# A transformer-like block of neighbourhood attention and three 3×3 convolutions: eight wait-carrying products dropped, the second convolution in full products plus one tap on row halves, and new orders on three engines

## What is computed

```python
q = jnp.einsum('bhwd,de->bhwe', x, Q_P)
k = jnp.einsum('bhwkd,de->bhwke', stk, K_P)
v = jnp.einsum('bhwkd,de->bhwke', stk, V_P)
scores = jnp.einsum('bhwke,bhwe->bhwk', k, q) * mask
alpha = jax.nn.softmax(scores, axis=-1)
attn = jnp.einsum('bhwk,bhwke->bhwe', alpha, v)
t = x + attn
t_in = t
t = jax.nn.relu(_conv(t, ff1_kernel, ff1_bias))
t = jax.nn.relu(_conv(t, ff2_kernel, ff2_bias))
t = jax.nn.relu(_conv(t, ff3_kernel, ff3_bias))
return t_in + t
```

## Time and profile before

| | |
|---|---|
| median of 3 runs | 2381.85 us (2379.44 to 2382.46) |
| the profiled execution | 2380.99 us, its span 2379.0 us |
| TensorE busy | 2287.5 us, 96% of the span |
| VectorE busy | 1895.5 us, 80% |
| ScalarE busy | 1127.4 us, 47% |
| mean granted TensorE clock | 0.993 of full speed |

### The profile page before, as it was taken

The page is one execution under the profiler, slowest core; times in us unless marked ns, Lnnn a source line. Parts: engine busy times, 40 slices in busy tenths (PEclk is TensorE's granted clock), DMA queues, the critical chain, the costliest instruction groups (busy, mean ns, idle before and its releaser), DMA issues.

```text
span 2379.0 us, 65460 instructions
## 1 busy us (share of the span) xinstructions
PE 2287.5 (96%) x25180; PEld 1317.7 (55%) x25180; DVE 1895.5 (80%) x2851; ACT 1127.4 (47%) x3108; POOL 15.5 (1%) x24
## 2 busy tenths in 40 slices
PE   4999999999999999999999999999998999999998
PEld 2655555555565555555555555555555555555554
DVE  4888888887588888888768888888877888888886
ACT  1554455444454554454345544544535445444543
POOL 2000000000000000000000000000000000000000
PEclk9999999999899999999999999999999999999999
DMA  4444544544355445444344454445434544454443
GB/s 125 138 137 136 158 134 125 160 141 134 94 158 152 137 126 162 139 136 137 123 138 144 126 160 140 135 136 157 135 124 119 156 147 138 127 160 136 128 153 119
DMA packets 291286, 328.79 MB, mean 138 GB/s; under 512 B 89300, under 2 KB 223252, under 8 KB 284564
## 3 DMA queue, kind: packets, MB, share of 16 engines
q1 hardware_dynamic: 291164, 327.17, 46.4%
HBM read 152.50 MB, written 33.82 MB: 78 GB/s over the span
## 4 chain that ended last, share of the span: by engine, by line
PE 79%; DVE 12%; issue 5%; ACT 1%; DVEq 1%; DMA 1%; SPq 0%; ACTq 0%
PE conv_banks L476 28%; PE conv_banks L435 16%; PE conv_banks L490 15%; PE mix_bank L413 6%; PE score_banks L387 3%; DVE work L836 3%; PE score_banks L398 3%; PE mix_bank L425 3%; DVE dt L764 2%; DVE tf L746 2%; DVE dt L760 2%; PE score_banks L381 1%; PE proj_bank L420 1%; PE score_banks L395 1%; PE conv_banks L450 1%
## 5 line engine op out<-in xcount | busy, mean ns | idle before, releaser
L476 PE MATMUL conv_banks<-dodd,w3f 128*64 128x512 f32 (+1 forms) x1656 | 500.3, 579 | 6.2 <-DVE dodd L760 3.9
L476 PE MATMUL conv_banks<-deven,w3f 128*64 128x512 f32 (+1 forms) x1656 | 489.9, 566 | 0.0
L598 ACT ACTIVATE prob<-score_banks,negmax 128x100 f32<-128x100 f32 x1040 | 343.0, 343 | 273.4 <-DVE negmax L726 273.4
L435 PE MATMUL conv_banks<-dt,w1f 128*64 128x256 f32 (+3 forms) x4224 | 414.4, 384 | 0.0
L490 PE MATMUL conv_banks<-duh,w2h 64*128 64x512 f32 (+2 forms) x1632 | 362.2, 423 | 4.0 <-ACT m_sb L634 2.1
L664 ACT ACTIVATE relued<-work,bias 128x1024 f32<-128x1024 f32 (+2 forms) x136 | 150.4, 1108 | 435.7 <-DVE work L836 435.7
L490 PE MATMUL conv_banks<-duh,w2l 64*128 64x512 f32 (+2 forms) x1632 | 329.5, 382 | 0.0
L435 PEld LDWEIGHTS conv_banks<-dt,w1f 128*64 128x64 f32 (+1 forms) x4224 | 219.2, 135 | 138.6 <-issue 65.9
L490 PE MATMUL conv_banks<-dul,w2h 64*128 64x512 f32 (+2 forms) x1632 | 286.4, 383 | 0.0
L476 PEld LDWEIGHTS conv_banks<-dodd,w3f 128*64 128x64 f32 x1656 | 138.8, 137 | 226.5 <-issue 181.3
L490 PEld LDWEIGHTS conv_banks<-duh,w2h 64*128 64x128 f32 x1632 | 168.7, 185 | 137.7 <-issue 104.5
(11 more groups left out here) (97 smaller groups left out, 3224.2 us busy)
## 6 DMA issues: line engine op xcount, KB each, us to landing
xk<-x_keys SPq DMA_DIRECT2D x66, 800.0 KB
xc<-x_bands SPq DMA_DIRECT2D x66, 650.0 KB, 5.0
dodd<-dodd SPq DMA_DIRECT2D x68, 512.0 KB, 5.1
xr<-x_bands SPq DMA_DIRECT2D x264, 128.0 KB, 3.5
out<-work SPq DMA_DIRECT2D x60, 512.0 KB, 2.7
dt<-dt SPq DMA_DIRECT2D x68, 256.0 KB, 2.3
deven<-deven SPq DMA_DIRECT2D x68, 256.0 KB, 5.7
duh<-duh SPq DMA_DIRECT2D x68, 256.0 KB, 2.4
```

What stands on the lines that cost most here:

```text
L435: mm = nc.tensor.matmul(bank[(LOWER, UPPER)[o], n * 256 + lo * 64:n * 256 + hi * 64], w1f[i][rows, m, s, o * C:o * C + C], dt[rows, lo + s ...
L476: return nc.tensor.matmul(bank[rows, lo * 128:hi * 128], w3f[:, m, s, odd * C:odd * C + C], source[:, lo + s // 2:hi + s // 2, m], start=s ...
L598: last = nc.scalar.activation(prob[:, g % 2, a], score_banks[:, g % 2, a * KEYS:(a + 1) * KEYS], ACT.Exp, bias=negmax[:, g % 2, a:a + 1], ...
```

## The change

1. **Waits.** In the loop's steps, the eight products of 2 columns are gone (`hold` keeps them in the prologue only). Their waits became `await_band`, `await_r`, `await_prob` and `await_y`, and stand ahead of a product of a convolution a little before the piece: `await_band` ahead of the last pair of the step before, `await_r(b, 0)` within the first convolution, `await_prob(b, 0)` and `await_r(b, 1)` ahead of the last two taps of a tile of the third, `await_prob(b, 1)` and `await_y` ahead of the last two products of `begin2`.
2. **Second convolution.** `begin2` issues four full products (128 rows) and `end2` two more, then six on row halves (three pairs). `go_on2` and `half_done` are gone.
3. **Orders.** TensorE: the tiles of the third convolution go 0, 1, 2, 3 (before 0, 2, 1, 3), `end2` of tiles 0 and 1 follow their own tile, `v_product` stands between `begin2` of tiles 2 and 3. ScalarE and VectorE: reordered as the diff shows.

Cut to its core, the diff of the helpers and of TensorE is:

```diff
 def fill_of(which, j):
-    return ORDER3.index(j) if which == CONV3 else 4 + 2 * j + (which == EVEN)
+    return j if which == CONV3 else 4 + 2 * j + (which == EVEN)
...
-                nc.tensor.matmul(score_banks[:, 0, 0:2], eye16_sb[:], window_sb[:, 0:2], start=True, stop=True)
...
+            def await_band(b):
+                pe.wait_ge(t_ready, b * 2)
+                pe.wait_ge(xc_in, b * 16 + 16)
+                pe.wait_ge(xs_in, b * 32 + 32)
...
                 for w in (w2h, w2l):
-                    tap2(k, EVEN, j, LOWER, 0, w, duh, w is w2h, False)
-                    tap2(k, ODD, j, UPPER, 0, w, duh, w is w2h, False)
-
-            def go_on2(G, k, j):
-                for w in (w2h, w2l):
-                    tap2(k, EVEN, j, LOWER, 1, w, duh, False, False)
-                    tap2(k, ODD, j, UPPER, 1, w, duh, False, False)
+                    if ahead and w is w2l:
+                        ahead()
+                    tap2(k, EVEN, j, FULL, 0, w, duh, w is w2h, False)
+                    tap2(k, ODD, j, FULL, 1, w, duh, w is w2h, False)
+
+            def end2(G, k, j, ahead=None):
+
                 pe.wait_ge(du_low, G * 2 + (j // 2 + 1))
-                for s in range(2):
-                    even = tap2(k, EVEN, j, LOWER, s, w2h, dul, False, False)
-                    odd = tap2(k, ODD, j, UPPER, s, w2h, dul, False, False)
-                even.then_inc(half_done, 1)
-                odd.then_inc(half_done, 1)
-
-            def end2(G, k, j):
-                pe.wait_ge(half_done, G * 8 + (2 * j + 2))
+                tap2(k, EVEN, j, FULL, 0, w2h, dul, False, False)
+                tap2(k, ODD, j, FULL, 1, w2h, dul, False, False)
                 for n, (w, d) in enumerate(((w2h, duh), (w2l, duh), (w2h, dul))):
-                    odd = tap2(k, ODD, j, LOWER, 1, w, d, False, n == 2)
-                    even = tap2(k, EVEN, j, UPPER, 0, w, d, False, n == 2)
+                    if ahead and n == 2:
+                        ahead()
+                    odd = tap2(k, ODD, j, UPPER, 0, w, d, False, n == 2)
+                    even = tap2(k, EVEN, j, LOWER, 1, w, d, False, n == 2)
...
                 conv3_tile(G, k, 0)
-                conv3_tile(G, k, 2)
+                conv3_tile(G, k, 1, (lambda: await_prob(b, 0)) if att else None)
                 if att:
                     turn(b, 0)
-                conv3_tile(G, k, 1)
+                conv3_tile(G, k, 2, (lambda: await_r(b, 1)) if att else None)
                 if att:
                     scores(b, 1)
                 conv3_tile(G, k, 3)
                 begin2(G, k, 0)
-                go_on2(G, k, 0)
+                end2(G, k, 0)
                 if att:
                     mix(b, 0)
-                begin2(G, k, 1)
-                go_on2(G, k, 1)
+                begin2(G, k, 1, (lambda: await_prob(b, 1)) if att else None)
                 if att:
                     turn(b, 1)
-                end2(G, k, 0)
                 end2(G, k, 1)
                 if att:
                     mix(b, 1)
-                begin2(G, k, 2)
+                begin2(G, k, 2, (lambda: await_y(b)) if att else None)
                 if att:
                     v_product(b)
-                go_on2(G, k, 2)
                 begin2(G, k, 3)
-                go_on2(G, k, 3)
                 end2(G, k, 2)
-                end2(G, k, 3)
+                next_band = None if k == BANDS - 2 else b if k == BANDS - 1 else b + 1
+                end2(G, k, 3, None if next_band is None else lambda: await_band(next_band))
```

In ScalarE's `step`:

```diff
+                if att:
+                    keep_r(b, 0)
                 if k:
                     relu_conv2(G, k - 1, ODD, 1)
-                if att:
-                    keep_r(b, 0)
-                if k:
                     relu_conv2(G, k - 1, EVEN, 1)
+                if att:
+                    keep_r(b, 1)
                 keep_u2(G, k)
                 if att:
                     exps(b, 0)
                     exps(b, 1)
-                    keep_r(b, 1)
+                keep_m2(G, k, CONV3)
                 relu_conv1(G, k)
-                keep_m2(G, k, CONV3)
```

and in VectorE's:

```diff
                 if k:
                     outer(G, k - 1, ODD, 1)
+                if k < BANDS:
+                    t_inputs(None, b - 1, k % 2, 1)
+                if k:
                     outer(G, k - 1, EVEN, 1)
                     inputs(G, k - 1, ODD, 0, 1)
                     inputs(G, k - 1, EVEN, 0, 1)
+                if att:
+                    max_scores(b, 0)
                 middle1(G, k)
                 if att:
-                    max_scores(b, 0)
+                    max_scores(b, 1)
+                outer1(G, k)
+                if att:
+                    scale(b, 0)
+                if k:
+                    inputs(G, k - 1, EVEN, 1, 1)
+                if att:
+                    scale(b, 1)
                 if k:
                     inputs(G, k - 1, ODD, 1, 1)
...
                 if att:
                     scale(b, 2)
+                u_low(G, k, 1)
+                if att:
                     scale(b, 3)
-                u_low(G, k, 1)
```

More of the change, by code:

```diff
@@ L449, in conv1 @@
                     pe.wait_ge(dve_read, outer_read(G, ODD, 1))
-                nc.tensor.matmul(conv_banks[:, 2 * outer, 0:2], eye16_sb[:], window_sb[:, 0:2], start=True, stop=True)
                 streams = (0, 3) if outer else (2, 1)
@@ L453, in conv1 @@
                     for i in range(2):
+                        if att and n == 1 and i == 1:
+                            await_r(b, 0)
                         for o in ((0,) if k == BANDS else (0, 1)):
@@ L589, in _ @@
                 step(g0 + BANDS, BANDS, b0 + BANDS, True)
-            for j in ORDER3:
+            for j in range(4):
                 conv3_tile(ALL_STEPS, 0, j)
@@ L870, in _ @@
             dve.wait_ge(w_ready, 3)
-            for part in range(2):
-                t_inputs(None, 0, 0, part)
+            t_inputs(None, 0, 0, 0)
             def step(G, k, b, par, att):
@@ L911, in step @@
                     add_x(k, b, par, 0)
-                    for part in range(2):
-                        t_inputs(G, b, par, part)
+                    t_inputs(G, b, par, 0)
                 if k == BANDS:
```

58 lines of the change are left out of this document (34 added, 24 removed).

## The result

| | before | after |
|---|---|---|
| median | 2381.57 us of 4 runs (2379.44 to 2382.46) | 2411.02 us of 4 runs (2408.31 to 2416.39) |
| ratio | | 1.0128, 95% interval 1.0109 to 1.0146 |
| span of the profiled execution | 2379.0 us | 2414.3 us |
| one full step (k = 2 to 14) | 34.69 us | 34.96 us |

The change makes the kernel 1.3% slower. The forecast was 2407 us. The profiled execution after is the slowest of its four, 5.4 us over the median. The engine table of the page, as in the earlier trace rows: TensorE has 2411 product records fewer (an fp32 product stands as two) and is busy 18 us longer.

What follows compares the result with a forecast made beforehand. TensorE's own stream was taken to bound the kernel. 52 full steps at +0.38 us (19.8) plus 3 and 3 us for other steps gave +26 us, so 2407 us; own range 2395 to 2418, overall range 2370 to 2424.

Steps and rivals of the forecast that it cites:

- Streaming of full products: Second convolution: a full product of 512 columns takes 0.235 us, as a half-row pair does, so streaming gains nothing.
- rival 1: Second convolution's full products stream in 0.216 us, −0.45 a step before longer waits; 2390 us in all; chance 0.22.
- A change between full and half rows: Second convolution: each shape change costs 0.10 drain plus 0.10 exposed weights, 0.20 us; five new ones a step, +1.00 us.
- Rival 2: No drain between full and half rows, so those switches cost nothing; 2355 us in all; chance 0.13.
- Second convolution with turn and V: Per full step: five shape changes +1.00, attention's second turn +0.19, V product without its hold −0.11 us.
- Dropped products ahead of it: Holds dropped before the second convolution: scores' halves −0.21 and −0.11, first convolution's outer half −0.11, first turn −0.16 us.
- Band start: At the R product only the hold behind the wait for VectorE goes; the rest is hidden: −0.11 us a step.
- Full step: Steps k = 2 to 14, 52 in all: shape changes, turn and dropped products sum to +0.38 us each, 19.8 us together.
- New orders, counted at nothing: Reordered engines: covers for the third convolution and second probabilities just suffice, 0 to 0.1 us wait for the latter; nothing added.
- Rival 3: VectorE's even ReLU or maximum 0.3 us late, delaying the third convolution: +0.3 × 52 on top, 2423 us; chance 0.10.
- Steps k = 0, 1 and 16: Twelve steps with shorter tiles and more waits that cover the same changes: +0.25 us each, +3 us in all.
- Steps without attention: Four k = 15 steps: seven switches, two fewer holds, +1.2 us; waits may hide 1.0; taken as +0.7 each, +3 us.

Runs made afterwards that it cites:

- experiment 1: The changed kernel with its second convolution back in half-row pairs, that convolution's tile order and ScalarE's tail as before: full step 34.10 us, 2353.36 us.
- experiment 2: The kernel before with only the eight wait-carrying products dropped, their waits put on other products, all old orders kept: full step 34.35 us, 2370.63 us.
- experiment 3: The changed kernel with tile 0's half rows behind tile 1's full products, tile 2's behind tile 3's, ScalarE's tail as before: full step 35.24 us, 2431.48 us.
- experiment 5: The changed kernel with the last two full products of tiles 2 and 3 together and both tiles' half-row pairs behind: full step 34.55 us, 2389.40 us.
- experiment 6: The changed kernel with one half-row pair ahead of the last two full products in every tile: full step 35.73 us, 2462.46 us.
- experiment 10: Experiment 3's kernel with VectorE's last scaling of the probabilities moved ahead of the second low part: full step 34.32 us, 2365.29 us.
- experiment 4: The changed kernel with the eight products of 2 columns put back at the head of their pieces, with their waits: full step 35.88 us, 2462.02 us.
- experiment 7: Experiment 1's kernel with VectorE's last scaling ahead of the second low part and orders in k = 16 and k = 15 mended: full step 33.88 us, 2336.50 us.
- experiment 8: The changed kernel with two orders undone outside the full steps only, in k = 15 and k = 16: full step 34.96 us, 2403.56 us.
- experiment 9: Experiment 7's kernel with the V product behind tile 2's first four streams instead of its first two: full step 33.36 us, 2304.39 us.

## Why the prediction was right, point by point

- **What bounds the kernel.** TensorE's stream did. VectorE and ScalarE have the same busy time in a step, and every edit of TensorE's stream came out in the step at its full size, unless a wait took its place (experiments 1, 2 and 3).
- **Streaming of full products, 0.235 us.** Right: 0.47 us for two. The lower bound 0.216, and with it rival 1 (2390), is out, and the surplus was not from two products side by side. The Trainium skill's isolated gap for 512 columns, about 216 ns (TensorE: Matmul & The Clock Gate, on the back-to-back issue gap), is not reached by full products either, with 235 ns here. For a sustained stream the same section of the Trainium skill gives 131 ns; the prediction did not weigh that figure, and no run here shows it.
- **A change between full and half rows, 0.20 us.** Right, and shown by three runs: 0.205 (experiment 5), 0.19 (6), 0.20 (10). The drain carried over from the weight loads of 64*64 holds for 128*128 and 64*128. Rival 2 (2355) is out: 0.56 and 0.34 stand where it wanted 0.47 and 0.235.
- **Second convolution with turn and V.** Forecast +1.00 + 0.19 − 0.11 = +1.08. From its first product to the last pair's start the step took 13.10 us before and takes 14.16 now: +1.06.
- **Dropped products ahead of it.** Forecast −0.59 from the first convolution's to the second's first product (−0.21, −0.11, −0.11, −0.16); measured −0.65 (19.65 to 19.00). The term that was mis-sized is the first turn: forecast 0.62 to 0.65 us, measured 0.58. The estimate had let the first transposed weights and the drain stand apart by more than they do.
- **Band start.** Forecast −0.11; from the last pair's start to the first convolution's first product 1.92 us before (1009.12 to 1011.04) and 1.80 after: −0.12.
- **Full step.** Forecast +0.38, measured +0.27: the parts add up to +0.28. 52 steps are 14 us instead of 19.8.
- **New orders, counted at nothing.** Nearly true of the change as it stands: in its full steps no wait for L820 shows, and that for the second probabilities is worth 0.04 us (experiment 10). But the covers named in the prediction were indeed thin. TensorE had only to come 0.9 us earlier for the second probabilities to leave it 0.66 us idle (experiment 3), and in experiment 1 they cost 0.22.
- **Rival 3,** VectorE's chain ahead of the third convolution, did not come true in the full steps. Its mechanism did in the last step of each pair, of which the prediction worked out no wait: there the first convolution is short, the ReLU stands behind the copy of R and a maximum before the sums, and the wait for L820 is 2.07 us where it was 0.59 (L803 before). Before, though, the scores had waited 0.57 us for R ahead of it, so the third convolution starts 6.54 us behind the R product instead of 5.97, and the second 18.86 instead of 18.62: the net cost is 0.2 us.
- **Steps k = 0, 1 and 16.** The term that was mis-sized most outside the full steps: forecast +0.25 each, 3 us for twelve; measured 7 us for the four k = 0 alone and 2 for k = 1. The forecast said that more waits there would cover the cost; they added to it. In k = 0, from the third convolution's first product to the second's, 7.66 us became 8.35: the waits for probabilities and turned probabilities now stand ahead of products that TensorE reaches too early, and put back at the head of their pieces they give 7.71 (experiment 4). From there to the next R product 11.76 became 13.29, and moving the last scaling in front of the low part takes 0.94 off this stretch (experiment 7 against 1). That the k = 0 differ from pair to pair comes from the first convolution: from its first product to the third's they take 12.85 to 14.13 us before and 12.56 to 13.31 after, with a mean granted clock of 0.91 to 0.95 over the step.
- **Steps without attention.** Also mis-sized: forecast +0.7 each, measured +1.5. "Waits there may hide 1.0" was wrong, since tile 3 now begins directly behind tile 2's start and the wait for VectorE's read grew from 0.46 to 1.45 us. Experiment 8 shows it: with this order undone, the steps 14 and 15 are 1.56 us shorter.
- **The sum.** +26 forecast, +29 measured. It is that close since the full steps were overrated by 6 us and the others underrated by 9: two errors of opposite sign, and in that part luck. What put the forecast on the right side was the price of a change of shape times its count.

## What to carry to other kernels

Count the changes of array shape in TensorE's order as one counts products. Here each cost 0.20 us, nearly the streaming of 512 columns, so that full products brought nothing over half-row pairs and their changes of shape took more (0.86 us a step, with their places) than the dropped products and new orders had saved (0.59). Dropping products that carry waits pays only as far as what they waited for is moved too: read for each wait how long its data has been ready, and reorder the engine that makes it. Look at the short steps of a loop apart; an order that is right in the long ones may put 1 to 2 us of wait into them.

## What was not expected of the hardware

- A wait in the middle of TensorE's stream costs more than the idle time that the profile shows beside it. An idle 0.25 us cost 0.52 (experiments 7 and 9), one of 0.22 cost 0.44 (experiment 2, the first convolution's part with the copy of R, against 1), one of 0.66 cost 0.92 (3 against 10), and one with no idle time shown cost 0.22 (1 against 7). The full step of the change itself has one: the second pair of tile 2, which waits for ScalarE's copy, starts 0.76 us behind the first (1050.03 to 1050.79) instead of 0.57, with 0.02 us shown as idle. The rows offer a reason: a product is shown as 0.4 to 0.5 us long, but the next one starts 0.235 behind it when nothing stops it. A stop first eats this overlap, some 0.2 us, before any idle time is seen. Start-to-start distances show it; the list of waits does not.
- A full fp32r product of 128*128 takes 0.235 us for 512 columns, the same as two half-row products side by side.
- The "issue" stall at the loop's return, 0.8 to 7.2 us over all these kernels, differs from pair to pair and from kernel to kernel with no edit near it. Its cause was not tried.
- Around the loop's return and in the short steps the granted clock falls to its lower level (1.2 GHz) for a while in every one of these kernels, in some pairs earlier than in others. In before's first pair it fell in k = 16 (mean granted clock of that step 0.86), behind waits of 0.16, 0.56 and 0.31 us, and the two halves of the V product start 0.90 us apart (621.72 to 622.62). The second pair has the same waits there, a mean of 0.99 and 0.48 us between the halves. Single short steps can therefore differ by 1 to 2 us for no edit; the steps in the middle of a pair agree within 0.02 us in each kernel.
